# Head as the inner index of the picked keys and values, and the third normalisation on ScalarE

## What is computed

```python
x = _layernorm(x + _L0_attn_ref(x, Wq, bq, Wk, bk, Wv, bv, Wo, bo))
x = _layernorm(x + _L0_xattn_ref(16, 256, 512, time_decay, time_first, x, ctx_2048))
x = _layernorm(x + _L0_ffn_ref(x, W_gate, W_qkv))

def _L0_ffn_ref(x, W_gate, W_qkv):
    gating = jax.nn.softmax(x @ W_gate.T, axis=-1)
    indicator = jax.nn.one_hot(jnp.argmax(gating, axis=-1), H)
    gating_top1 = indicator * jnp.max(gating, axis=-1, keepdims=True)
    q, k, v = jnp.split(x @ W_qkv.T, 3, axis=-1)
    k = k.reshape(Bb, Tt, H, hd)
    v = v.reshape(Bb, Tt, H, hd)
    k_shared = jnp.einsum('bth,bthd->btd', indicator, k)
    v_shared = jnp.einsum('bth,bthd->btd', gating_top1, v)
    att = jnp.einsum('bhqd,bkd->bhqk', q, k_shared) * (1.0 / math.sqrt(hd))
    ...
```

## Time and profile before

| | |
|---|---|
| median of 3 executions | 1896.69 us (1890.73 to 1903.83) |
| the profiled execution | 1906.39 us, span 1904.6 us |
| mean granted clock of TensorE in it | 0.918 of 2.4 GHz |
| TensorE matmuls busy | 1561.5 us, 82% |
| VectorE busy | 1271.8 us, 67% |
| ScalarE busy | 551.4 us, 29% |
| GpSimd busy | 517.7 us, 27% |

### The profile page before, as it was taken

The page is one execution under the profiler, slowest core; times in us unless marked ns, Lnnn a source line. Parts: engine busy times, 40 slices in busy tenths (PEclk is TensorE's granted clock), DMA queues, the critical chain, the costliest instruction groups (busy, mean ns, idle before and its releaser), DMA issues.

```text
span 1904.6 us, 33047 instructions
## 1 busy us (share of the span) xinstructions
PE 1561.5 (82%) x11392; PEld 1273.4 (67%) x11392; DVE 1271.8 (67%) x2679; ACT 551.4 (29%) x1168; POOL 517.7 (27%) x701
## 2 busy tenths in 40 slices
PE   4668879888888888888888888889888887988746
PEld 4556667777666777766667676667767666776534
DVE  3356685757768676776868677685867668585744
ACT  2232232323323232232323233232323223232211
POOL 1033051322405132230514233051413305142220
PEclk8678999999999989989999999989999898999869
DMA  5212132221223222122322213132221313222010
GB/s 140 89 56 71 48 84 62 61 60 42 78 50 83 61 56 64 42 78 50 83 61 63 62 37 86 42 83 61 64 64 35 87 39 83 61 64 59 19 45 12
DMA packets 61493, 118.28 MB, mean 62 GB/s; under 512 B 12688, under 2 KB 31120, under 8 KB 61456
## 3 DMA queue, kind: packets, MB, share of 16 engines
q1 hardware_dynamic: 61456, 117.79, 24.3%
HBM read 32.81 MB, written 8.39 MB: 22 GB/s over the span
## 4 chain that ended last, share of the span: by engine, by line
PE 49%; DVE 31%; issue 9%; DMA 4%; POOL 3%; ACT 1%; DVEq 0%; SPq 0%; POOLq 0%; ACTq 0%
PE pp L396 11%; PE pp L397 9%; PE pp L398 9%; DVE neg_max L1068 6%; DMA q_stack<-max_rows 3%; DVE neg_parts L1072 3%; PE sq L437 3%; PE po L502 2%; DVE w_val L1255 2%; PE sk L464 2%; PE sq L429 2%; PE po L488 2%; DVE o_tok L1104 2%; PE sk L472 1%; DVE w_key L1164 1%
## 5 line engine op out<-in xcount | busy, mean ns | idle before, releaser
L849 ACT ACTIVATE prob<-sk 128x512 f32<-128x512 f32 x384 | 215.7, 596 | 541.6 <-PE sk L467 330.0
L1068 DVE TENSOR_REDUCE neg_max<-sq 128x2 f32<-128x512 f32 (+1 forms) x384 | 249.6, 677 | 56.6 <-PE sq L432 31.7
L396 PE MATMUL pp<-xt_hi,w_hi 128*128 128x256 f32 x768 | 232.5, 303 | 27.3 <-DVE w_lo L1055 13.8
L397 PE MATMUL pp<-xt_lo,w_hi 128*128 128x256 f32 x768 | 222.4, 290 | 0.0
L398 PE MATMUL pp<-xt_hi,w_lo 128*128 128x256 f32 x768 | 222.1, 289 | 0.0
L396 PE MATMUL pp<-w_hi,xt_hi 128*128 128x512 f32 x384 | 169.9, 442 | 29.7 <-DVE w_val L1255 25.4
L1103 DVE RECIPROCAL o_rec<-po 128x8 f32<-128x8 f32 x128 | 25.9, 203 | 228.9 <-PE po L502 228.3
L396 PEld LDWEIGHTS pp<-xt_hi,w_hi 128*128 128x128 f32 x768 | 152.5, 199 | 35.0 <-issue 21.8
L1486 POOL TENSOR_TENSOR xt_lo<-x_raw,xt_hi 128x1024 fp32r<-128x1024 f32 x16 | 38.0, 2376 | 445.4 <-ACT xt_hi L898 445.4
L397 PE MATMUL pp<-w_lo,xt_hi 128*128 128x512 f32 x384 | 159.0, 414 | 0.0
L398 PE MATMUL pp<-w_hi,xt_lo 128*128 128x512 f32 x384 | 158.6, 413 | 0.0
(11 more groups left out here) (162 smaller groups left out, 3784.5 us busy)
## 6 DMA issues: line engine op xcount, KB each, us to landing
q_stack<-q_hi SPq DMA_DIRECT2D x256, 128.0 KB, 2.3
q_stack<-q_lo SPq DMA_DIRECT2D x128, 128.0 KB, 2.3
k_stack<-k_hi SPq DMA_DIRECT2D x128, 128.0 KB, 2.3
x_raw<-in_xT SPq DMA_DIRECT2D x16, 512.0 KB, 3.5
k_stack<-k_lo SPq DMA_DIRECT2D x64, 128.0 KB, 2.3
xa<-in_x SPq DMA_DIRECT2D x16, 512.0 KB, 3.4
w_val<-in_ctxT SPq DMA_DIRECT2D x64, 128.0 KB, 2.1
out_y<-xb SPq DMA_DIRECT2D x16, 512.0 KB, 2.9
```

The source lines that it names most:

```text
L396: T.matmul(out, lh, rh, start=(c == 0), stop=False, skip_group_check=True)
L397: T.matmul(out, lh, rl, start=False, stop=False, skip_group_check=True)
L849: A.activation(dst, sk[n % 2][:], ACT.Exp, scale=SCALE).then_inc(s_exp, 1)
L1068: V.tensor_reduce(dst, src, AX.X, ALU.max, negate=True).then_inc(s_max, 1)
```

## The change

Two things are changed.

The rows of the key and value matrices of the gated attention are laid out with the head as the inner index (`heads_inner`, on the host), so that the projection leaves the 16 heads' channels of one position side by side in `pp`. `picked` has the same order, the indicator is broadcast over the outer index, and the reduce sums 16 neighbours 32 times, where it summed 16 elements that lie 32 apart.

The third normalisation is written as `x * rstd + bias` with `bias = -mean * rstd`. GpSimd computes the bias in two more operations (`third_bias`), and ScalarE applies it (`third_norm`); VectorE's `ln_apply(2, ...)` goes.

```diff
-        picked = w_val[:].rearrange("p c t -> p (c t)").rearrange("p (h d) -> p h d", h=NH)
+        picked = w_val[:].rearrange("p c t -> p (c t)").rearrange("p (d h) -> p d h", h=NH)
...
+            def third_norm(b):
+
+                act.wait_ge(ln_biased, b + 1)
+                for c in range(TT):
+                    e = A.activation(xb[:, c, :], xb[:, c, :], ACT.Identity, scale=rstd[:, 2, c:c + 1],
+                                     bias=ln_bias[:, c:c + 1])
+                e.then_inc(x3_ready, 1)
...
                     value_out(t, 1)
+                if prev and not (isinstance(t, int) and t < 2):
+                    third_norm(t - 2)
+                if do_a:
                     copy_a(t, 0)
...
-                V.tensor_tensor(picked, pp[:].rearrange("p (h d) -> p h d", h=NH),
-                                g_ind[:, c, :].unsqueeze(2).to_broadcast([P, NH, HD]), ALU.mult).then_inc(pf_free, 1)
+                V.tensor_tensor(picked, pp[:].rearrange("p (d h) -> p d h", h=NH),
+                                g_ind[:, c, :].unsqueeze(1).to_broadcast([P, HD, NH]), ALU.mult).then_inc(pf_free, 1)
                 dve.wait_ge(pf_free, PF_JOBS * b + job + c + 1)
-                ch.link(V.tensor_reduce(dst[:, c, :], picked.rearrange("p h d -> p d h"), AX.X, ALU.add))
+                ch.link(V.tensor_reduce(dst[:, c, :], picked, AX.X, ALU.add))
...
-                if prev and not (isinstance(t, int) and t < 2):
-                    ln_apply(2, t - 2, xb, xb, x3_ready)
...
-            ln_apply(2, NB - 1, xb, xb, x3_ready)
...
-                pool.wait_ge(pool_ln[n], b + 1)
+                pool.wait_ge(pool_ln[n], 2 * b + 1 if n == 2 else b + 1)
                 G.tensor_tensor(rstd[:, n, :], var_eps[:, n, :], minus_half[:], ALU.pow).then_inc(ln_rstd[n], 1)
+
+            def third_bias(b):
+
+                G.tensor_tensor(neg_mean[:], meanvar[:, 2, :, 0], minus_one[:], ALU.mult).then_inc(pool_ln[2], 1)
+                pool.wait_ge(pool_ln[2], 2 * (b + 1))
+                pool.wait_ge(ln_rstd[2], b + 1)
+                G.tensor_tensor(ln_bias[:], neg_mean[:], rstd[:, 2, :], ALU.mult).then_inc(ln_biased, 1)
...
                 if prev:
                     inverse_std(t - 1, 2)
+                    third_bias(t - 1)
                 products(t, 3)
...
+    def heads_inner(w):
+
+        return w.reshape(NH, HD, -1).transpose(1, 0, 2).reshape(D, -1)
+
-            quadrants(wqkv[0:D]), wqkv[D:2 * D], wqkv[2 * D:3 * D]]
+            quadrants(wqkv[0:D]), heads_inner(wqkv[D:2 * D]), heads_inner(wqkv[2 * D:3 * D])]
```

More of the change, by code:

```diff
@@ L139, in build @@
         minus_half = sb("minus_half", [P, TT])
+        minus_one = sb("minus_one", [P, TT])
+        neg_mean = sb("neg_mean", [P, TT])
+        ln_bias = sb("ln_bias", [P, TT])
         logit = sb("logit", [P, TT, NH])
@@ L212, in build @@
         pool_ln = [sem(f"pool_ln{n}") for n in range(3)]
+        ln_biased = sem("ln_biased")
         def slot(n):
@@ L1045, in _ @@
             iteration(NB, False, True, False)
+            third_norm(NB - 1)
         @block.vector
@@ L1449, in _ @@
             V.tensor_tensor(gate_lo[:], gate, gate_hi[:].bitcast(f32), ALU.subtract)
+            V.memset(minus_one[:], -1.0)
             V.memset(minus_half[:], -0.5).then_inc(consts, 1)
@@ L1584, in _ @@
             inverse_std(NB - 1, 2)
+            third_bias(NB - 1)
 def kernel(**inputs):
```

## The result

The changed kernel took 1913.94 us (median; 1893.74 to 1924.45) against 1896.69 us (1890.73 to 1905.57), a ratio of 1.0074 with a 95% interval of 1.0042 to 1.0106. The profiled execution took 1920.74 us with a span of 1918.9 us and a mean granted clock of 0.913 (before: 1906.39, 1904.6 and 0.918). The forecast was 1898, with 1877 to 1917 as its range: the time is in the range, but 16 us above the forecast.

The account below looks back on a forecast made before the run. One chain of waits, 49% TensorE and 31% VectorE, was taken to bound the kernel. Terms -6.4 + 6.9 + 1.0 = +1.5 us gave 1907.9 profiled, 1898 on the median's scale, range 1877 to 1917.

Parts of the forecast that it names:

- The pick: VectorE's reduce in each pick: from 1090 ns to 0.69 us by reading neighbours, saving 0.40 us; -6.4 us over 16 iterations.
- Rival 1: The pick's reduce stays at 1.09 us because short sums cost, not the step; 1904.5 us, chance 0.10.
- only one saving of four counts: Key picks end in idle time, the two value picks are parallel branches: one 0.40 us saving per iteration.
- GpSimd's operations: Two new operations between the pow and the last products, on the chain of waits: 0.46 us, 15 iterations, +6.9 us.
- Rival 2: GpSimd's two operations cost near the pow's price, 1.40 us instead of 0.46: +14.1 us, 1912, chance 0.06.
- ScalarE's part: Third normalisation on ScalarE fits idle time before L860, pair at most 1.6 us, 0.7 left; only the end costs, +1.0 us.
- The collision stays: VectorE's value-pick cast still held by GpSimd's subtraction, since both move by 0.40 us; 13 or 14 long casts, term 0.
- So I expect the same mixture: TensorE's clock: 0.4 us of idle time removed and 0.46 added elsewhere leave the mix of steady periods as it was.
- the sum of +1.5 us: Whole kernel: pick -6.4, GpSimd's operations +6.9, bare cost at the end +1.0 us.
- The bounds: Clock spread over 13 steady periods: -24.8 us if all were as short as the shortest, +23.3 if all at 112.9.
- Rival 3: Added wait at 1161 to 1164 drops TensorE's clock every iteration: 1921 us; passes 1% at about nine of 13; chance 0.12.
- The clock criterion of the forecast: Whole profile: the forecast would be wrong if the mean granted clock moves by over 0.01.

Follow-up runs that it names:

- the fillers: Ten extra unread matmuls per iteration, put into two TensorE waits of the kernel before: 1878.99 us, ratio 0.9891; in the changed kernel 1879.42 us, 0.9892.
- the layout alone: The kernel before with only the head-inner layout of the picks, normalisation left on VectorE and no new GpSimd operations: 1925.22 us, ratio 1.0146.
- late split: The kernel before with ScalarE's x_split_hi(t + 1) moved behind copy_f(b, 0): 1872.03 us, ratio 0.9850.

## Why the prediction came out as it did

**The pick** was right: 0.69 forecast, 0.686 measured. The Trainium skill (VectorE: DVE Perf Modes, Mode 1× (REGULAR) — the baseline) gives the plain mode one result per cycle and names no price of a stride; these rows show one. Rival 1 is out. That only one saving of four counts is shown by the 0.38 us between the first value reduce and GpSimd's subtraction (8.38 to 8.00) and by the 12.87 us ahead of it, which the two key picks leave as they were.

**GpSimd's operations** were right: 0.46 us forecast, 0.46 more in the steady wait (1.00 to 1.46). Rival 2 is out.

**ScalarE's part** was right: 1.51 us for the pair, and idle time left ahead of the o_ch copy, 1.33 us where the forecast had 0.7. VectorE's wait for the attention output grew, as expected, from 228.9 us on the page of before to 264.9; where the normalisation stood it is 3.55 us for 2.65 (3.7 forecast), and behind the first key pick and the first value pick it took up their savings (1.97 to 2.37 us and 1.68 to 2.12). At the end 1.52 us took the place of 1.00, with 0.46 on GpSimd ahead.

**The collision stays** was right, 14 casts ("13 or 14").

**"So I expect the same mixture"** is the step that failed, and with it the sum of +1.5 us, against 14 to 17 measured. The reasoning was that 0.4 us of idle time taken from one place and 0.46 put into another leave the clock alone. They moved the low stretches from 7, 13 and 7 of 13 iterations to 12, 13 and 12, which is the 16.7 us. The bounds (-24.8 us, -24.7 by the rows, and +23.3) were well placed: the fillers gave back 23.3 us of the 13 iterations of the kernel before (1444.4 to 1421.1), and the edits alone made them 18 us longer (1462.4 with the layout alone). Why differences of 0.4 us tip the pattern stays open. That the time still fell into the range is the merit of the range, which was drawn from the clock's spread, and partly luck: it lies 3 us inside the upper end.

**Rival 3** had the outcome nearly (periods towards 112.9) and the place as well, with a chance of 0.12. The idle stretch some 6 us behind the added wait is the one ahead of the third place, and in 12 of 13 iterations the clock now falls there and, in the next one, behind the collision. Its cause wasn't borne out: the layout alone adds no wait on GpSimd, and both places are low in nearly every iteration of it. Its threshold is off too: 23.3 us over the ten periods that were not yet so make 1% pass at about eleven of the 13, not nine. What rows 11 offered was the warning that counts: 3.7 us between iterations with the same instructions, against terms of 0.4 us. With a mixture like that, its chance should have been nearer to that of the forecast. The clock criterion of the forecast (the mean moves by over 0.01) was too coarse: it moved by 0.005.

## What to carry to other kernels

Before summing terms of 0.4 us, lay the steady iterations side by side with their low-clock stretches. If they differ by more than the terms, the outcome can hang on which pattern the edit tips the loop into, and a single part measured alone doesn't add up with the others. Price a small edit on a version in which TensorE's waits are filled; and try fillers for their own sake, since ten matmuls without a reader were worth 1 to 1.5% here. Where a VectorE instruction (here a cast) is held by GpSimd in each iteration, try to move what releases GpSimd behind the next copy.

## What was not expected of the hardware

The granted clock fell behind waits of 1.56 and 1.63 us in a TensorE that was busy for 83% of the span (late split). The price of a stretch depends on its place: 6.8 us of low clock cost 0.46 us at the second place (109.21 against 108.75, though the fillers themselves are in the latter), and 3.4 us cost 1.5 at the first, where TensorE has projections without a wait. The Trainium skill (TensorE: Matmul & The Clock Gate, HAM oscillation — how this bites in real kernels) tells of a loop that drops its clock behind a DMA wait in every turn; here it is so in each of 13 iterations at the second place, behind a wait of 1.65 us for the copies of the keys in the one from 1105.34. That loops settle on the same lengths from different work (109.2 us in three kernels, 112.6 in five) is seen, and not explained by these runs. The two lengths lie 3.4 us apart, as long as the shortest low stretch; whether that is more than chance was not tested.
